# C rows of a scan chunk: from TensorE's selection matmuls to broadcast transfers and ScalarE copies

## The reference, cut to what matters

```
h   = relu(adj @ layernorm(x) @ gcn_w + gcn_b); h = layernorm(h)*ln_g + ln_b
xc, z = split(h @ w_in)                       # 256 + 256 channels
u   = silu(conv4(xc) + conv_b)
dbc = u @ w_xp                                # dt (8), B (16), C (16) for each token
dt  = softplus(dbc[:, :8] @ w_dt + b_dt)
# scan over the 8192 tokens, 16 states for each of the 256 channels:
hst = exp(dt*A) * hst + dt*B*u ;  y = sum over states of hst * C
x   = x + ((y + u*D_skip) * silu(z)) @ w_out
x   = x + lstm_layer(layernorm(x))            # LSTM over the tokens and prefix/suffix sums
```

## Time and profile before

| what | value |
|---|---|
| three runs | 1649.15 us median, 1646.19 to 1650.54 |
| profiled execution | 1649.25 us; span from first to last instruction 1647.4 us |
| TensorE busy | 1534.2 us, 93% of the span; granted clock 0.974 over the span, 1.00 in the steady chunks |
| VectorE busy | 1437.4 us, 87% |
| GpSimd busy | 1114.7 us, 68% |
| ScalarE busy | 980.2 us, 60% |
| 16 DMA engines | 317.17 MB, busy share 0.7 to 0.8 until about 1180 us, then near nothing |

### The profile page before, as it was taken

How to read it: one execution, slowest core, us unless ns; L and a number is a source line. 1 busy time by engine, 2 the same in 40 slices (tenths; PEclk the granted TensorE clock), 3 DMA queues, 4 the chain that set the end, 5 groups by cost and what they waited for, 6 DMA issues and landing times.

```text
span 1647.4 us, 18204 instructions
## 1 busy us (share of the span) xinstructions
PE 1534.2 (93%) x5212; PEld 794.1 (48%) x5212; DVE 1437.4 (87%) x1640; ACT 980.2 (60%) x2051; POOL 1114.7 (68%) x518
## 2 busy tenths in 40 slices
PE   6999999999999999999999999999967669999994
PEld 2444444444444444444444444444422227999993
DVE  8406999999999999999999999999987894558998
ACT  2254766667575766666676757576657444555552
POOL 4014998989898988989898989889867860001221
PEclk9999999999999999999999999999978898999997
DMA  8977767777777777777777777777500203000002
GB/s 309 358 241 263 272 232 254 251 244 257 246 251 258 246 253 242 255 250 247 250 256 240 250 263 241 251 255 253 183 13 8 89 7 109 0 0 1 0 0 102
DMA packets 62649, 317.17 MB, mean 193 GB/s; under 512 B 6898, under 2 KB 6898, under 8 KB 29684
## 3 DMA queue, kind: packets, MB, share of 16 engines
q1 hardware_dynamic: 49680, 293.30, 51.2%
q10 hardware_dynamic: 12900, 23.08, 4.8%
HBM read 304.03 MB, written 12.32 MB: 192 GB/s over the span
## 4 chain that ended last, share of the span: by engine, by line
PE 62%; DVE 24%; issue 9%; ACT 2%; POOL 1%; DVEq 1%; ACTq 0%; DMA 0%; POOLq 0%
PE bank L526 39%; DVE work L1143 11%; PE bank L446 10%; PE bank L451 4%; DVE work L1093 4%; PE bank L555 3%; PE bank L571 3%; DVE work L1166 2%; DVE work L1101 1%; PE bank L562 1%; PE bank L564 1%; DVE work L1197 1%; DVE work L1065 1%; POOL work L943 1%; DVE work L1202 1%
## 5 line engine op out<-in xcount | busy, mean ns | idle before, releaser
L526 PE MATMUL bank<-ring,xh 128*128 128x512 f32 x2048 | 951.8, 593 | 15.8 <-DVE xh L1031 15.8
L1143 DVE TENSOR_TENSOR_SCAN work<-bank,hstate,work 128x512 f32<-128x512 f32 x512 | 627.7, 1267 | 17.0 <-ACT bank L787 12.7
L526 PEld LDWEIGHTS bank<-ring,xh 128*128 128x128 f32 x2048 | 389.4, 190 | 463.3 <-issue 436.8
L922 POOL TENSOR_TENSOR work<-work 128x1024 f32<-128x1024 f32 x210 | 502.7, 2394 | 88.2 <-DVE work L1101 82.6
L787 ACT ACTIVATE bank<-work,a_neg 128x512 f32<-128x512 f32 x512 | 346.8, 687 | 303.1 <-DVE work L1143 302.3
L1093 DVE TENSOR_TENSOR work<-work,bank 128x1024 f32<-128x1024 f32 x256 | 309.9, 1215 | 26.6 <-PE bank L451 16.0
L446 PE MATMUL bank<-work,w_sb 128*128 128x512 f32 (+2 forms) x352 | 181.8, 614 | 20.4 <-ACT work L777 10.2
L993 POOL TENSOR_TENSOR work<-work 128x256 f32 x32 | 28.5, 891 | 240.1 <-ACT work L826 240.1
L1101 DVE TENSOR_TENSOR work<-work,bank 128x1024 f32<-128x1024 f32 x154 | 184.2, 1196 | 1.3
L451 PE MATMUL bank<-bc_parts,sel 96*128 96x512 bf16 x442 | 168.2, 391 | 16.0 <-DVE work L1093 7.0
L882 POOL TENSOR_TENSOR work<-work 128x1024 f32<-128x1024 f32 x48 | 113.6, 2367 | 80.9 <-ACT work L679 80.7
(11 more groups left out here) (144 smaller groups left out, 1635.8 us busy)
## 6 DMA issues: line engine op xcount, KB each, us to landing
ring<-adj_t SPq DMA_DIRECT2D x256, 1024.0 KB, 4.9
work<-c_scratch ACTq DMA_DIRECT2D x35, 256.0 KB, 4.4
c_two<-c_scratch ACTq DMA_DIRECT2D x35, 256.0 KB, 4.3
xh<-x_rows SPq DMA_DIRECT2D x16, 256.0 KB, 5.9
work<-x_t SPq DMA_DIRECT2D x16, 256.0 KB, 5.1
x_scratch<-work ACTq DMA_DIRECT2D x16, 256.0 KB, 5.1
work<-x_scratch SPq DMA_DIRECT2D x1, 4096.0 KB, 13.6
out_t<-work SPq DMA_DIRECT2D x16, 256.0 KB, 2.7
```

Of the source, the lines that this page charges most:

```text
L526: last = nc.tensor.matmul(mixed[:, :], xn[:, j, :], a, start=(j == 0), stop=(j == BLK - 1))
L922: nc.gpsimd.tensor_tensor(out=acc, in0=hc[0] if n == 1 else acc, in1=hc[n % 2], op=ALU.add).then_inc(y_added, 1)
L1143: nc.vector.tensor_tensor_scan(hb[s % 2][:, h, :], da[h], dbu[s % 2][:, h, :], hstate[:, HV * s + h:HV * s + h + 1], ALU.mult, ALU.add).th ...
```

## The change

Before, TensorE spreads the eleven C rows that VectorE multiplies, and only GpSimd's five rows come by broadcast load. After, all sixteen rows of a chunk come by broadcast load, issued by ScalarE, row s in step s (row 15 with row 14 in step 14), to the two `c_rows` buffers in turn. For the eleven rows of VectorE, ScalarE copies the buffer to the PSUM bank that TensorE filled before (`place_c`), one step behind the load. GpSimd reads its five rows from the buffers as before. A load waits until its buffer's last row has been used: by GpSimd's product, or by ScalarE's own copy. A copy waits for its row to land, and for VectorE's last product from the bank. In the draining chunks (14 and 15) nothing changes. At k = NC the load of the LSTM's bias rows, which uses the second buffer, waits for the copy of row 15 of chunk 13 in place of GpSimd's last product.

```diff
-C_LOAD = {0: 1, 2: 3, 6: 8, 8: 10, 12: 14}
...
                 def spread_c(n):
-                    if drains(k):
-                        if cs == NC - 2 and n == 0:
-                            pe.wait_ge(hc_done, hc_count(cs - 1, DS - 1, False))
-                        else:
-                            pe.wait_ge(c_copied, DS * (cs - (NC - 2)) + n)
-                    elif n in POOL_HC:
-                        return
-                    elif n >= 2:
-                        wait(pe, hc_done, hc_count(cs, n - 2, False))
-                    elif not (isinstance(cs, int) and cs == 0):
-                        pe.wait_ge(hc_done, hc_count(cs - 1, DS + n - 2, False))
-                    spread(c_bank, c_ready, DS + n, 0 if drains(k) else n)
+                    if cs == NC - 2 and n == 0:
+                        pe.wait_ge(hc_done, hc_count(cs - 1, DS - 1, False))
+                    else:
+                        pe.wait_ge(c_copied, DS * (cs - (NC - 2)) + n)
+                    spread(c_bank, c_ready, DS + n, 0)
...
                 for s in range(16):
-                    if scan and not drains(k) and s >= 1:
-                        spread_c(s - 1)
...
-                if scan and not drains(k):
-                    spread_c(DS - 1)
...
                 if isinstance(k, int) and k == NC:
-                    act.wait_ge(pool_hc_done, len(POOL_HC) * (NC - 2))
+                    act.wait_ge(c_ready, c_spreads(NC - 3, DS - 1))
                     act.dma_start(bias_rows, lstm_bias).then_inc(bias_loaded, 16)
...
                 def load_c(n):
 
-                    i = POOL_HC.index(n)
-                    b = (par + i) % 2
+                    b = n % 2
                     act.wait_ge(c_stored, 16 * (cs + 1))
-                    wait(act, pool_hc_done, hc_count(cs, n, True) - 2)
+                    m, c = (n - 2, cs) if n >= 2 else (n + DS - 2, cs - 1)
+                    if c >= 0 and m in POOL_HC:
+                        act.wait_ge(pool_hc_done, hc_count(c, m, True))
+                    elif c >= 0:
+                        act.wait_ge(c_ready, c_spreads(c, m))
                     act.dma_start(c_rows[b], c_dram[cs, n:n + 1, :].broadcast_to([P, CH])).then_inc(c_row_in[b], 16)
+
+                def place_c(n):
+
+                    act.wait_ge(c_row_in[n % 2], 16 * (DS // 2 * cs + n // 2 + 1))
+                    m = max([x for x in range(n - 1) if x not in POOL_HC and x % 2 == n % 2], default=None)
+                    if m is not None:
+                        act.wait_ge(hc_done, hc_count(cs, m, False))
+                    elif cs > 0:
+                        act.wait_ge(hc_done, hc_count(cs - 1, DS - 1, False) - (n == 0))
+                    nc.scalar.activation(c_bank[n % 2][:, :], c_rows[n % 2], ACT.Copy).then_inc(c_ready, 1)
...
-                    if scan and not drains(k) and s in C_LOAD:
-                        load_c(C_LOAD[s])
+                    if scan and not drains(k):
+                        if s >= 1 and s - 1 not in POOL_HC:
+                            place_c(s - 1)
+                        if s < DS - 1:
+                            load_c(s)
+                        if s == DS - 2:
+                            load_c(DS - 1)
...
                 if scan and drains(k):
                     copy_c(DS - 1)
+                elif scan:
+                    place_c(DS - 1)
...
                     else:
-                        i = POOL_HC.index(n)
-                        b = (par + i) % 2
-                        pool.wait_ge(c_row_in[b], 8 * (len(POOL_HC) * cs + (i - b)) + 16)
-                        c = c_rows[b]
+                        pool.wait_ge(c_row_in[n % 2], 16 * (DS // 2 * cs + n // 2 + 1))
+                        c = c_rows[n % 2]
```

## The result

The kernel before runs in 1648.9 us, the changed one in 1701.6 us (four runs each, 1646.19 to 1650.54 and 1692.53 to 1711.47): a ratio of 1.032, interval 1.028 to 1.037. It is slower by 52.8 us, where 26 were forecast. The spread is itself a finding: 1.1% from run to run, against 0.3% before. The profiled execution of the changed kernel is its fastest, 1692.53 us, so it shows 43 of the 53 us.

A forecast was written before the change was run, and what follows sets the result against it. VectorE and TensorE were taken as full, with ScalarE full in steps 8 to 11. The profiled 1649.25 us plus 28 for landing waits minus 2 at k = 16 gave 1675; range 1645 to 1705.

The forecast's parts named there:

- It waits for the landing: ScalarE's stream: each copy, one step behind its load, waits for the row, delaying that step's work and the next exponentials.
- I take +2.0: 14 x 2.0 = 28 us: Landing waits on ScalarE: 2.0 us a chunk over the 14 changed chunks, 28 us in all.
- The walk: Steps 5 to 10 followed with 4.4 us landings: copies 5, 7, 9 wait; L1059 and all behind it +2.3 us.
- In the last steps ScalarE waits for VectorE again, so nothing is added: End of the chunk, behind L1059: no further loss and nothing given back, so the +2.3 us stays.
- the prediction's own line for 4.9 us: The same sum over a chunk's steps with landings of 4.9 us: +3.7 us a chunk, 1699 us.
- Copy 9: Steps 9 to 10: load 9 lands at 715.4, its copy could start at 714.3; L718 starts 2.3 us late.
- rival 3: DMA engines crowd, landings of 5 to 6 us: 1699 us at 4.9, 1756 at 5.9; chance 0.13.
- no relief of TensorE is worth over 1.03 us a chunk: VectorE's wait for "out" at L1059 caps the gain: about 14 us over 14 chunks, unless VectorE's work shrinks.
- the order argument: "dbc", "dt0", "dt1" and "out" follow in order between TensorE and ScalarE: best case -0.2 us a chunk.
- Rival 2: VectorE's wait at L1059 for "out" goes altogether: -1.03 x 14 - 2 = -16, 1633 us; chance 0.10.
- Most of it falls into idle time before exponentials: ScalarE's eleven copies, 5.5 us a chunk, mostly cost nothing; cover is missing in steps 8 and 10.
- the wait at k = 16: The bias load's wait for GpSimd's fourteenth product, holding L777, goes once: 1.7 us gained, taken as 2.

The follow-up runs named there:

- e4: The changed kernel with four row buffers in place of two, each load one step earlier except row 15's: 1649.9 us, ratio 1.001.
- e16: The changed kernel with rows 5, 7, 9 and 15 spread by TensorE again, seven copies left: 1651.4 us, ratio 1.002.
- e14: The changed kernel with row 15 alone spread by TensorE again, neither loaded nor copied: 1682.2 us, ratio 1.022.
- e1: The kernel before without the eleven spreads from the second scan chunk on, nothing in their place (wrong C values): 1618.9 us, ratio 0.983.
- e9: The kernel before with GpSimd's sum of state 10 moved behind its step-12 subtraction: 1632.4 us, ratio 0.990.
- e11: The changed kernel with four row buffers, loads one step earlier, and GpSimd's sum of state 10 behind its step-12 subtraction: 1616.1 us, ratio 0.982.
- e2: The kernel before with ScalarE's eleven copies a chunk from a constant tile replacing the spreads, no new loads: 1652.7 us, ratio 1.002.
- e3: The kernel before, spreads kept, with eleven more broadcast loads a chunk into spare buffers that nobody reads: 1650.7 us, ratio 1.001.
- e8: The changed kernel with row 7 alone spread by TensorE again, its load and copy gone: 1692.2 us, ratio 1.028.
- e13: The changed kernel, two row buffers, with GpSimd's sum of state 10 behind its step-12 subtraction: 1710.3 us, ratio 1.035.

## Why the prediction was half right

**The direction and the mechanism**: right. "It waits for the landing", in ScalarE's stream, in front of the exponentials: shown by e4, where the same traffic with more distance costs nothing, by e16, where four rows fewer do the same, and by the rows of the chunk.

**The size: the term that failed** is "I take +2.0: 14 x 2.0 = 28 us"; it measured 52 (e4 against the changed kernel), 3.7 a chunk. The walk took 4.4 us for every landing and found three waiting copies, 5, 7 and 9. What these three cost came out near the 28 forecast, some 31 us (e14 against e16, in this one order of taking rows away). The largest part that was missing is row 15; the landings and the clock come with it.
- Row 15, the step that failed: "In the last steps ScalarE waits for VectorE again, so nothing is added" was false. Load 15 goes out with load 14, its copy waits in 13 of 14 chunks, and it stands in front of what TensorE needs first. Taking it off gave 19 us (e14); rows 5, 7 and 9 with it, 50 (e16).
- The landings: 4.7 to 4.8 us in the median of loads that used to take 4.3 and 4.4, and not one number but a spread that goes with the place. Load by load, the medians of the rows run from 3.2 (row 12) and 3.3 (row 11) over 5.6 (row 15) to 6.8 (row 9) and 7.1 (row 4). By the prediction's own line for 4.9 us, +3.7 a chunk, the sum would have been 1699; that this line fits is in part luck, for it has no row 15 in it.
- The clock: a stand of 3 us on TensorE costs a further 1.8 us in its next six matmuls at half clock (4.72 instead of 2.90). The forecast had no such term. The Trainium skill, "TensorE: Matmul & The Clock Gate", Part 1, says that activity is what releases the throttle and an idle engine falls back to half; the rows above agree.

Copy 9 was luck. Its load takes 6.8 us in the median, far over the 4.4 of the walk, but goes out some 3 us earlier than the walk had it. So copy 9 waited in only 5 of 14 chunks, 4.4 us in all. The waits of copies 2 and 4, 18.3 us, were not in the walk either; rows 2 and 4 keep 17.6 us of waits in e16 and cost next to nothing there. The Trainium skill, "DMA: Bandwidth & Descriptors", section Anatomy of one DMA, gives the fit behind the 2.6 us for transfers that GpSimd issues; ScalarE issues these, and no run shows 2.6, the shortest landing being 3.0.

The range held the median, which says little, since it reached from no change to twice the forecast; rival 3 (1699 at landings of 4.9) was nearer than the forecast, and it had 0.13.

**TensorE's relief**: "no relief of TensorE is worth over 1.03 us a chunk, unless VectorE's own work shrinks. It doesn't." This is the wrong step that mattered most for understanding, though not for the number. Taking the spreads away was worth 2.4 us a chunk (e1). The bound of 1.03 itself held, with 0.8 where the best case of the order argument was 0.2. What failed is "It doesn't": VectorE's busy time did shrink, because 1.9 us of it in every chunk was standing behind GpSimd. The earlier trace rows shows 73.98; in e1 it is 72.4, in e9 72.2 and in e11 72.1. The Trainium skill, "SBUF — State Buffer", section Who interferes with whom, has the rule: a VectorE instruction with two SBUF inputs contends with a GpSimd one that reads SBUF, and the port pair that they share is an exclusive lock. The rows agree in both orders, 3.12 and 2.35 us, 1.54 and 3.22. Rival 2's price, 16 us, was half of what was there.

**The copies' cost**: "Most of it falls into idle time before exponentials" and "costs nothing" holds nearly in e11 and failed in e2, by 34 us. It is near the truth as long as no lateness of "out" changes who is first at L1065.

**What stayed as said**: ring loads stand the traffic (e3); the first load's wait for GpSimd's product 14 is there in ten chunks of twelve, 1.6 us at most, where 1.5 was forecast; the wait at k = 16 gave 2.0 us. The busy time of VectorE stayed at 74 and TensorE's came to 72.8 at full clock, near the 72 forecast.

**What stays open**: how the 0.8 us by which "out" came earlier in e1 split between an earlier "dbc" and "dt0", and why one row lands in 3.2 us and another in 7.1; that a ring load or another row close by is the cause is likely, but not shown. No run varied the ring loads' place.

## What to carry to other kernels

When a load's wait stands in the stream of an engine that others depend on, give each load its own landing time, by its place among the other transfers, and take the long end for those that stand in front of a shared engine's next work; a second pair of buffers (e4) took nearly all of these waits away. Before taking a "full" engine at its busy time, compare the single durations of one line: an instruction that lasts 3.1 us in one place and 1.2 in another is waiting, and moving the neighbour may be worth more than the change at hand (here 17 us for one addition). An edit that shifts an engine by half a microsecond can decide which of two engines goes first and which stands, so measure parts of a change in the setting in which they will run.

## What the runs showed of the hardware

- VectorE's L1065 (two SBUF inputs, 128x1024 f32): 1.22 us alone, 3.12 behind a GpSimd addition that began 0.32 us earlier, 1.54 when it began 0.52 us ahead of that addition, which then took 3.22 instead of 2.35. The same for a product with its C row in SBUF: 1192 ns at least, 2182 in the median; from PSUM 1198. Where VectorE stood, it ended 1.1 us behind GpSimd's end.
- A 256 KB broadcast load lands after 3.0 to 9.6 us, the same instruction in the same program, with medians of 3.2 to 7.1 us by its place in the chunk.
- ScalarE's queue can issue a load ahead of activations that stand before it in the code: load 9 at 890.24, the exponentials before it at 893.21.
- After a 3.00 us stand TensorE's four matmuls took 3.08 us instead of 1.88, at a granted clock of 0.50.
- With the waits the time is uneven: the changed kernel spreads by 1.1% from run to run, e8 by 1.5% and e13 by 1.7%, the kernel before by 0.3% in four runs and 0.5% in the most that were taken beside an experiment (24). The profiled chunks run from 77.8 to 81.9 us where each was 75.7 before.
